# Another table for the order of steps in a two-block windowed-attention kernel

## The reference

```python
xn = layer_norm(x) * g + b
win = windows(pad(xn))                  # 14x14 windows, 4 to an image
q, k, v = split(win @ qkv_w + qkv_b)    # 12 heads of 16 channels
attn = (q * 16 ** -0.5) @ k.T + rel_h + rel_w   # rel_* from q and two tables
x = x + unwindow(softmax(attn) @ v @ proj_w + proj_b)
h = gelu((layer_norm(x) * g2 + b2) @ fc1_w + fc1_b)
x = x + h @ fc2_w + fc2_b
```

## Time and profile before

| | |
|---|---|
| three runs | 577.96, 581.3 and 584.08 us, median 581.3 us |
| the profiled execution | span 581.3 us |
| busy share of the span | PE 90%, PEld 80%, DVE 64%, ACT 46%, POOL 23% |
| chain that ended last, by engine | PE 66%, SP's queue 11%, "issue" 7%, DMA 6%, DVE 6%, ACT 3% |
| mean granted TensorE clock | 0.938 of full speed |

### The profile page before, as it was taken

How to read it: one execution, slowest core, us unless ns; L and a number is a source line. 1 busy time by engine, 2 the same in 40 slices (tenths; PEclk the granted TensorE clock), 3 DMA queues, 4 the chain that set the end, 5 groups by cost and what they waited for, 6 DMA issues and landing times.

```text
span 581.3 us, 12103 instructions
## 1 busy us (share of the span) xinstructions
PE 522.1 (90%) x4448; PEld 462.9 (80%) x4448; DVE 372.1 (64%) x924; ACT 269.3 (46%) x524; POOL 133.7 (23%) x317
## 2 busy tenths in 40 slices
PE   2868799989999998999999998999899999898866
PEld 2856678878899887888888898888798888777646
DVE  3347566766777686766777776867677666755220
ACT  2121342545646365635546463646455545445602
POOL 1222121313213141402223131414141212311200
PEclk9857586999999999989999999999999999979988
DMA  6542422041422321220403121212213040401100
GB/s 163 139 137 79 134 68 81 1 132 42 123 78 80 108 80 54 67 67 2 130 3 100 33 79 55 80 54 68 66 32 101 2 132 1 132 3 40 46 15 14
DMA packets 29758, 40.97 MB, mean 70 GB/s; under 512 B 5795, under 2 KB 14467, under 8 KB 29699
## 3 DMA queue, kind: packets, MB, share of 16 engines
q1 hardware_dynamic: 29699, 40.20, 23.8%
HBM read 6.57 MB, written 1.57 MB: 14 GB/s over the span
## 4 chain that ended last, share of the span: by engine, by line
PE 66%; SPq 11%; issue 7%; DMA 6%; DVE 6%; ACT 3%; POOL 1%; DVEq 0%; ACTq 0%; POOLq 0%
PE back L817 11%; PE by_key L968 10%; PE times_v L978 8%; PE by_query L953 7%; SPq L309 6%; PE front_b L817 6%; PE front_b L923 6%; PE front_a L923 5%; PE back L1028 4%; PE front_a L817 4%; DMA pad_t<-pad_pack 3%; DMA q_stack<-rel_lo 3%; DVE rel_lo L710 2%; ACT probs L526 2%; SPq L300 2%
## 5 line engine op out<-in xcount | busy, mean ns | idle before, releaser
L756 DVE TENSOR_REDUCE row_max<-by_query 128x2 f32<-128x512 f32 x192 | 132.3, 689 | 87.0 <-PE by_query L953 85.1
L526 ACT ACTIVATE probs<-by_key 128x512 f32<-128x512 f32 x192 | 106.9, 594 | 82.7 <-PE by_key L968 68.2
L953 PE MATMUL by_query<-k_stack,q_stack 108*128 108x256 f32 x384 | 89.5, 316 | 9.6 <-DVE row_max L756 4.6
L968 PE MATMUL by_key<-q_stack,k_stack 110*128 110x256 f32 x384 | 79.7, 310 | 8.4 <-ACT probs L526 8.3
L968 PEld LDWEIGHTS by_key<-q_stack,k_stack 110*128 110x128 f32 x384 | 55.9, 192 | 26.1 <-ACT probs L526 13.3
L953 PEld LDWEIGHTS by_query<-k_stack,q_stack 108*128 108x128 f32 x384 | 63.7, 200 | 13.7 <-issue 7.2
L1028 PE MATMUL back<-w,hid 128*128 128x192 f32 x384 | 71.6, 326 | 0.0
L350 POOL TENSOR_TENSOR norm_rstd<-norm_var,minus_half 128x2 f32<-128x2 f32 x32 | 22.8, 713 | 177.5 <-DVE norm_var L634 166.6
L1028 PEld LDWEIGHTS back<-w,hid 128*128 128x128 f32 x384 | 61.3, 190 | 0.3
L817 PE MATMUL back<-xn_hi,w_hi 128*128 128x256 f32 x192 | 55.7, 301 | 3.3 <-ACT hid L544 1.7
L817 PE MATMUL back<-xn_hi,w_lo 128*128 128x256 f32 x192 | 52.6, 286 | 0.0
(11 more groups left out here) (133 smaller groups left out, 979.6 us busy)
## 6 DMA issues: line engine op xcount, KB each, us to landing
k_stack<-k_hi SPq DMA_DIRECT2D x32, 192.0 KB, 2.9
q_stack<-q_hi SPq DMA_DIRECT2D x32, 192.0 KB, 3.1
q_stack<-rel_hi SPq DMA_DIRECT2D x32, 168.0 KB
q_stack<-rel_lo SPq DMA_DIRECT2D x32, 168.0 KB
q_stack<-q_lo SPq DMA_DIRECT2D x16, 192.0 KB, 2.7
k_stack<-k_lo SPq DMA_DIRECT2D x16, 192.0 KB, 2.8
X<-in_x SPq DMA_DIRECT2D x8, 192.0 KB, 3.1
k_stack<-av_t SPq DMA_DIRECT2D x8, 192.0 KB
```

The lines of the kernel that those rows point to most:

```text
L526: act.activation(probs[h % NP], KB[h % 2][:, :].rearrange("p (k t) -> p k t", k=2), ACT.Exp).then_inc(s_ex, 1)
L756: dve.tensor_reduce(row_max[:, h, :], QB[:, :].rearrange("p (a t) -> p a t", a=TILES), AX, ALU.max).then_inc(s_smax, 1)
L953: last = pe.matmul(QB[:, a * TOK:(a + 1) * TOK], q_stack[n % 2][0:ROWS_Q, h, a * P:(a + 1) * P], k_stack[n % 2][0:ROWS_Q, h, :], start=Tru ...
L968: last = pe.matmul(KB[h % 2][:, c * TOK:(c + 1) * TOK], k_stack[n % 2][0:ROWS_K, h, c * P:(c + 1) * P], q_stack[n % 2][0:ROWS_K, h, :], st ...
```

## The change

PERIOD and every number of PLACE are replaced (the new numbers are on a scale ten times finer). No step, instruction, wait or buffer changes: only the order in which each engine goes through its steps.

```diff
-PERIOD = 4497
+PERIOD = 44970
 PLACE = {
...
-    "gelus": (104237,), "front_rest": (0, 94723), "stats0": (73757,), "hat0": (76787,), "low0": (80533,),
...
+    "gelus": (1046168,), "front_rest": (809189, 956237), "stats0": (774943,), "hat0": (799232,), "low0": (813131,),
...
 }
```

More of the change, by code:

```diff
@@ L81 @@
+    "top_transposes": (893762,),
+    "by_key": (902439, 903172, 905781, 906402, 908697, 910789, 917251, 918290, 921546, 926248, 927277, 927536),
+    "times_v": (917180, 932065, 941067), "back_products": (851802, 942171), "to_tokens": (944976,),
+    "att_transposes": (947902,), "projection": (951070,), "transpose1": (966617,), "fc1": (974907, 975125, 978011),
+    "fc2": (979882, 980726, 981708, 981887, 984617, 985130),
 }
```

43 lines of the change are left out of this document (19 added, 24 removed).

## The result

After: 537.50 us median of 4 runs (536.64 to 542.16). Before: 580.05 us (577.96 to 584.08). The ratio is 0.929, 95% interval 0.925 to 0.933. The forecast was 553.2 us with a range of 540 to 572: right in sign, 16 us short in size, and outside the range.

A forecast was written before the change was run, and what follows sets the result against it. PE, busy 90% of the span, was taken to bound the kernel, so only its waits and low clock could be won. Middle 16.5, start 8.9 and end 2.7 us sum to 28.1, so 581.3 becomes 553.2 us, range 540 to 572.

The forecast's parts named there:

- the middle: 13 turns from 98.71 to 509.15 us: 21.8 us of PE waits go, 5.3 us of new ones come, 16.5 us gained.
- new waits: Middle: DVE's packed stretch at the turn's end may make PE wait 0.4 us a turn, 5.3 us in all.
- The three groups: PE's waits in the middle for `tops` (9.7 us), an exponential (5.9 us) and the last rel_lo DMA (1.6 us).
- Cost 0: ACT: exps 10 and 11 behind gelus and a table load take 3.8 us, 1.2 us to spare before `times_v 2`.
- ACT ties two images together: Rival: exponentials wait behind another image's gelus, so `times_v 2` and `q_products` come late in 14 turns; 587 us, chance 0.06.
- The normalisation: Start: first image's normalisation done before 11 us, so `q_products` starts at 13.7 us; 3.5 us gained.
- `back_products`: Start: block 0's costs 4.6 us at its new place and saves 6.15 us at the old one; 1.6 us gained.
- the other two terms: Start: less idle time from 39.27 to 65.65 us, 2.4 us, and from 65.65 to 98.71 us, 1.4 us.
- The clock comes back earlier: Rival: from 65.65 to 98.71 us PE returns to full clock, 7 of 8.8 us come in; 546 us, chance 0.14.
- Weights late: Rival: moved `back_products` waits on PE for its weights ahead of the first `by_query`; 560 us, chance 0.05.
- the waits come back elsewhere: Rival: PE's order nearly without slack, 1.3 us of new waits a turn, middle gains 5 us; 566 us, chance 0.18.
- the two cases without a gain: Rivals: only the first image's gain, 578 us, chance 0.05; slower through ACT's new order, 587 us, chance 0.06.

The follow-up runs named there:

- b_key: Kernel before with by_key of head 2 moved behind att_transposes and by_query of head 2; ratio to before 0.985.
- a_key: Kernel after with by_key of heads 1 and 2 put back directly behind head 0; ratio to before 0.956.
- b_sp: Kernel before with SyncE's queue alone in the new order, the scatter ahead of the next image's stacks; ratio to before 1.027.
- b_pads: Kernel before with the pads' chain earlier on every engine it crosses (seven numbers), stacks in their old order; ratio to before 0.974.
- a_many: Kernel after with pad_products, by_key of head 6 and by_query of head 10 moved, 14 F32-to-F32R changes a turn instead of 11; one run, 541.8 us.
- a_norm: Kernel after with front_rest, VectorE's work on the first layer's weights, ahead of everything again; ratio to before 0.939.
- a_back: Kernel after with back_products and back_rest at their old place, in the second image's turn; ratio to before 0.940.
- a_one: Kernel after with by_key of head 8 behind transpose1, 10 F32-to-F32R changes a turn instead of 11; one run, 542.7 us.
- b_pads_key: Kernel before with the pads' chain earlier and by_key of head 2 behind by_query of head 2 (eight numbers); ratio to before 0.957.
- x_PEA: Kernel before with the pads' chain earlier, after's TensorE order except back_products, second times_v_out later, and after's ScalarE order; ratio to before 0.967.
- x_PE: Kernel before with the pads' chain earlier, after's TensorE order except back_products, and second times_v_out later; ratio to before 1.097.

## Why the prediction was right or wrong

**The step that failed is the middle: 16.5 us forecast, 33.1 measured.** The working was 21.8 us of waits less 0.4 us a turn of new ones, 5.3 us. Put right:
- The waits counted went, 21.8 us, by the causes named: `by_key` by b_key and a_key, `tops` by b_sp and b_pads.
- The new waits are 0, not 5.3 us: PE is busy for all of 377.37 us. The price was a guess without a row, and it took a quarter of what the waits give.
- The three groups of the earlier trace rows hold 17.2 us of idle time, but the earlier trace rows show 19.4, in 35 places: with 0.16 us of overlap for each, 25.0 us. That is 3.2 us more. Half of it is one wait that the prediction reckoned into the end, 1.55 us ahead of the last image's `by_query 0`.
- 3.4 us of the middle of before are at half clock (258.3 to 261.7 us), worth 1.7 us; "at full clock" was a rounded 1.00. That none are in after is in part luck: in the turn with block 1's `back_products` the clock fell behind the one-column products in before, a_key and a_many, and did not in after, a_norm, a_back and a_one.
- The remaining 6.4 us (33.1 - 21.8 - 3.2 - 1.7), 0.49 us a turn, are busy time. The TensorE's own order, 0.3 to 0.5 us a turn by b_pads_key against after and x_PEA, is most or all of it. The prediction said "the same PE work stands in the same turn" and took the same work for the same time.

The wait that the prediction reckoned into the end, in before:

```profile
509.15 0.47 PE L953 MATMUL by_query<-k_stack,q_stack 108*128 108x256 f32 x2 [1.55 <-DMA q_stack<-rel_lo]
```

**The scatter.** "The scatter now stands ahead of the stack DMAs, and `pads_total`, on which it waits, stands some three heads earlier on DVE": right (by the tables `pads_total` moves over four row maxima, and `pads_top` over five), and b_sp shows that the second half carries the first. Without it the same queue order makes the kernel 2.7% slower.

**ACT.** Cost 0: right, no `times_v` waits in after. Where the term fell short is that this reorder was priced only as a cost. x_PE shows what it is for: without it the new PE order loses 3.0 us and then the clock, in every turn. The rival in which ACT ties two images together had the right engine and the opposite sign: the new ACT order removes a wait.

The row of a table load in after is 1.28 us, and the next activation starts 1.30 us after the load's start, as in the earlier trace rows. The load itself starts as soon as the activation before it ends (402.04 + 0.84 us), and no `times_v` waits:

```profile
402.04 0.84 ACT L544 ACTIVATE hid<-back,b 128x256 f32<-128x256 f32 x2 [1.78 <-PE back L817]
402.89 1.28 ACT L526 ACT_TABLE_LOAD   x1
404.19 0.60 ACT L526 ACTIVATE probs<-by_key 128x512 f32<-128x512 f32 x1
```

The Trainium skill (ScalarE: Activation LUTs, "What ACT_TABLE_LOAD costs") adds a drain to every switch of tables. These rows leave no room for one on either side.

**The start**, 8.9 us forecast and 11.1 measured, was near stretch by stretch, as far as two profiles can tell whose starts may differ by 2 to 3 us without any edit. To the first `by_query`: a loss of 1.1 (3.5 less 4.6) forecast, 0.1 measured. From there to the second image's: 2.4 forecast, 3.2 measured. To the third's: 1.4 and the 6.15 of `back_products`, 7.55 forecast, 8.0 measured. The terms behind these sums did not all hold. The normalisation was sized well: 3.5 us forecast, 3.7 measured (a_norm, beside its later first product). `back_products` was mis-sized: 1.6 us forecast, but with it back at its old place the start is 8.0 us longer in the profile and the median 8.45 us (a_back), with 54.6 us at half clock instead of 37.5. The term was the products' own time alone; that the clock could come back earlier without them stood among the rivals. The two come to 11.7 us, as much as the whole start gained, and leave nothing for the other two terms (3.8 us forecast), which no run took apart. So the nearness of the sum is partly luck. The normalisation is a small part of the change: 0.5% alone in before, and 0.939 against 0.929 when undone in after.

**The end**, 2.7 us forecast and 0.8 measured. Counted from the last image's `by_query 0`, `projection` of that image comes 2.6 us earlier than before; then the clock falls to half 0.7 us ahead of its start (at 513.7 us; in before at 562.0, 0.9 us behind its start), and 1.8 us are given back by the last `fc2`.

**The rivals.** "The clock comes back earlier" happened in part, by these two profiles: 51.2 us at half clock in the start became 37.5, and the record's first time at full moved from 22.7 to 18.8 us. "Weights late" and "the waits come back elsewhere" did not, nor did the two cases without a gain.

## What to carry to other kernels

A gain in an order is counted from the bounding engine's idle time in the stretch (here 19.4 us and its overlaps), not from the largest groups of waits alone; what that leaves out (here 8 of 33 us) is the clock, and the pace at the borders of steps, which an order also sets. A price for "new waits" needs a row that names the waiting step. An engine's new order can cost time without the orders it was made for: SyncE's alone cost 2.7%, the TensorE's without ScalarE's 9.7%, and both are part of a gain of 7.1%. Work of a few columns was cheaper in a stretch that was at half clock anyway (a_back against after, 0.940 and 0.929).

## What the runs showed of the hardware

- The clock row of a page says 1.00 ahead of the first change it recorded, also where PE ran at half. In after the row says 1.00 from 0 on, and the record begins at 18.8 us. Products of one shape start 0.21 us apart up to there and 0.11 us behind it:

```profile
18.43 0.41 PE L817 MATMUL front_b<-qkv_hi,xn_hi 128*128 128x192 f32 x1
18.64 0.36 PE L817 MATMUL front_b<-qkv_lo,xn_hi 128*128 128x192 f32 x1
18.83 0.27 PE L817 MATMUL front_b<-qkv_hi,xn_lo 128*128 128x192 f32 x1
18.94 0.27 PE L817 MATMUL front_b<-qkv_hi,xn_hi 128*128 128x192 f32 x1
```

  So PE ran at 1.2 GHz until then (in before until 22.7 us, where the spacing changes alike), and the clocks of the earlier trace rows for the first stretch are too high.
- A wait of 3.0 us in a turn that is otherwise full went with a clock at half for 3.4 us in every turn of x_PE; with a wait of 0.7 us in each turn (a_key) the clock fell in one of 13.
- DVE is 18.5 us busier in after (390.6 against 372.1) with the same instructions. Part of this is one of the two rel_lo steps, which in each turn takes 1.89 us where it runs beside two POOL instructions (1.04 in before); the other runs alone and takes 0.68 us. POOL's cast takes 1.07 us there and 0.60 in before. It lies beside PE's work, and no PE wait in the middle goes with it:

```profile
425.70 1.89 DVE L710 TENSOR_TENSOR rel_lo<-rel_full,rel_hi 84x512 fp32r<-84x512 f32 x1
...
431.62 0.68 DVE L710 TENSOR_TENSOR rel_lo<-rel_full,rel_hi 84x512 fp32r<-84x512 f32 x1
```
```profile
426.04 1.00 POOL L426 TENSOR_TENSOR X<-X,b 128x384 f32<-128x384 f32 x1
426.98 1.07 POOL L363 CAST rel_hi<-rel_full 84x512 fp32r<-84x512 f32 x1
```
- The first F32R step behind an F32 product is longer (`by_key` 0.32 us instead of 0.24), but behind transposes and `fc2` products PE loses nothing by it, since the step before is shorter by the same. Three more such changes in a turn cost 0.27 us in all, two of them all of it (a_many).
